# A graph layer's edge stage with its engines a whole batch apart, gathers and scatters mixed, and loads over 128 partitions

## What is computed

```python
deg = maximum(zeros(N).at[dst].add(1.0), 1.0)
edge_weight = (deg[src] * deg[dst]) ** -0.5
edge_msg = relu(edge_attr @ W1e + b1e) @ W2e + b2e
messages = (x[src] + edge_msg) * edge_weight[:, None]
agg = segment_sum(messages, dst, N)
combined = (1.0 + gin_eps) * x + agg
h = relu(combined @ W1n + b1n) @ W2n + b2n
out = h + x
out = out * rsqrt(mean(out * out, -1) + 1.19e-07) * rms_w
return layernorm(x + out)
```

## Time and profile before

| | us |
|---|---|
| median of 3 runs (2165.39 to 2170.3) | 2165.47 |
| the profiled execution, its own time | 2150.24 |
| span of that execution in the trace | 2148.5 |
| mean granted TensorE clock | 0.856 |
| PE, DVE, ACT, POOL busy in the span | 1537.2, 1290.7, 1118.8, 1303.8 |
| count stage, about | 25 to 316 |
| list set-up | 316 to 340 |
| edge stage | 340 to 1478 |
| node stage | 1484 to 2148 |

### The profile page before, as it was taken

The page is one execution under the profiler, slowest core; times in us unless marked ns, Lnnn a source line. Parts: engine busy times, 40 slices in busy tenths (PEclk is TensorE's granted clock), DMA queues, the critical chain, the costliest instruction groups (busy, mean ns, idle before and its releaser), DMA issues. The chain is left out here.

```text
span 2148.5 us, 43403 instructions
## 1 busy us (share of the span) xinstructions
PE 1537.2 (72%) x11484; PEld 1127.5 (52%) x11484; DVE 1290.7 (60%) x4579; ACT 1118.8 (52%) x3879; POOL 1303.8 (61%) x2171
## 2 busy tenths in 40 slices
PE   1114995666666667666666677775999999999993
PEld 0002554544545445445545566664777777777772
DVE  2003996333334334343333466662999999999997
ACT  1003982222222222222222244444999999999994
POOL 5772002555555555555555545553588888888888
PEclk8556997688787886877877899997999999999997
DMA  7793001212212112111111112114366666666662
GB/s 284 302 412 144 0 3 31 53 54 53 53 53 54 53 53 54 54 53 53 53 53 53 52 56 58 59 61 183 128 252 248 234 242 248 253 253 234 235 246 115
DMA packets 83038, 275.63 MB, mean 128 GB/s; under 512 B 19110, under 2 KB 46300, under 8 KB 58396
## 3 DMA queue, kind: packets, MB, share of 16 engines
q1 hardware_dynamic: 57422, 231.16, 29.2%
q0 software_dynamic: 25136, 43.60, 6.9%
q10 hardware_dynamic: 414, 0.20, 0.0%
HBM read 154.37 MB, written 128.22 MB: 132 GB/s over the span
## 5 line engine op out<-in xcount | busy, mean ns | idle before, releaser
L542 POOL DMA_INDIRECT agg_scratch<-scaled,sca_i x390 | 387.6, 994 | 576.6 <-ACT scaled L661 484.2
L1022 PE MATMUL bank<-digits,picks 128*128 128x128 f16 x5488 | 441.1, 241 | 211.7 <-DVE picks L772 121.0
L1022 PEld LDWEIGHTS bank<-digits,picks 128*128 128x128 f16 x5488 | 382.6, 110 | 319.3 <-issue 165.3
L535 POOL DMA_INDIRECT xs<-in_x,src_x x391 | 377.5, 965 | 132.4 <-issue 118.8
L886 DVE TENSOR_TENSOR msg<-bank,xs 128x512 f32<-128x512 f32 x98 | 67.8, 692 | 549.7 <-issue 536.2
L575 POOL TENSOR_SCALAR xsc<-xn,rms 128x128 f32<-128x128 f32 x784 | 277.9, 370 | 128.9 <-ACT rms L684 125.5
L655 ACT ACTIVATE he<-bank,b1e_c 128x512 f32<-128x512 f32 x98 | 67.5, 689 | 512.7 <-remote 433.3
L587 POOL TENSOR_SCALAR on<-z,neg_mean,rstd 128x128 f32<-128x128 f32 x588 | 257.2, 445 | 0.0
L1000 PE MATMUL bank<-oh_hi,steps 128*128 128x512 f16 x392 | 143.6, 406 | 144.1 <-issue 125.8
L1049 PE MATMUL bank<-w2e,he 128*128 128x128 f32 x784 | 163.2, 374 | 111.9 <-ACT he L655 111.9
L1078 PEld LDWEIGHTS bank<-w2n,hn 128*128 128x128 f32 x1568 | 205.8, 191 | 70.2 <-issue 64.6
(11 more groups left out here) (145 smaller groups left out, 2601.2 us busy)
## 6 DMA issues: line engine op xcount, KB each, us to landing
agg_scratch<-zeros SPq DMA_DIRECT2D x48, 1024.0 KB
xn<-in_x SPq DMA_DIRECT2D x48, 1024.0 KB
ag<-agg_scratch SPq DMA_DIRECT2D x48, 1024.0 KB, 6.8
out<-on SPq DMA_DIRECT2D x48, 1024.0 KB, 4.9
highq<-src_high_scratch SPq DMA_DIRECT2D x98, 128.0 KB
ea<-in_edge_attr SPq DMA_DIRECT2D x97, 127.0 KB
xs<-in_x,src_x POOLq DMA_INDIRECT x391
agg_scratch<-scaled,sca_i POOLq DMA_INDIRECT x390
```

Source lines behind the costliest of these rows:

```text
L535: pool.indirect_dma_start(out=xs[:, b % XS, j, :], out_offset=None, in_=x, in_offset=bass.IndirectOffsetOnAxis(ap=src_x[:, t:t + 1], axis= ...
L542: pool.indirect_dma_start(out=agg_rows, out_offset=bass.IndirectOffsetOnAxis(ap=sca_i[:, t:t + 1], axis=0), in_=scaled[:, b % 2, j, :], in ...
L1022: last = pe.matmul(ps[s][:, j * P:(j + 1) * P], picks[:, s, c, j * P:(j + 1) * P], digits[:, d, c * P:(c + 1) * P], start=c + d == 0, stop ...
```

## The change

1. **Start-up loads.** src and dst are loaded over all 128 partitions for the columns 0 to 342 and, for the 48 columns behind them, as 112 and as 15 partitions (ROWS = 112). The previous partition's last dst (column 0 of dst_x) comes by SP, later; the next partition's first dst is part of the wider load. Only the parts that no load covers are padded first. ACT casts dst to float after the count stage.
2. **Bias.** b2 is loaded as a row on three partitions and split in three bf16 parts there by DVE, after the count loop; PE's transposes of it (L990) go.
3. **Zero stores.** Three semaphores; each store first waits for the one three before it (ZERO_FIRST is 8 instead of 12).
4. **Gathers.** XS is 40, so 160 gathers stand ahead of the first scatter. Eight slots (32 to 39) first hold the temporaries of the list set-up, so gather 128 waits for lists_ready. The other 231 gathers are spread singly over the first 362 scatters; the last DRAIN = 7 batches have none.
5. **Steps.** In step b PE turns ea(b), counts b, multiplies by W1e, and does bias and W2e of b - 1. ACT does eaT(b), weighs b - 3, he(b), ds(b - 2), and scales b - 5, in a loop of four steps. DVE picks b + 1, does the degrees of b - 1, sums b - 4 and adds msg of b - 2; DVE and SP are written out whole, with constants for registers. `scaled` has SR = 4 buffers instead of 2.
6. **Loads.** edge_attr comes in one DMA of 128 partitions for batches below 85, then as 112 + 15. xn loads wait for 78 instead of 84 batches' msg; the first ag block comes in four pieces with a semaphore each.

```diff
-    XS = 32
+    XS = 40
+    SR = 4
+    TEMPS = 8
+    DRAIN = 7
+    ROWS = (P - 1) // 16 * 16
...
+        temps = [xs[:, XS - TEMPS + k, :, :].rearrange("p j d -> p (j d)")[:, 0:T] for k in range(TEMPS)]
+        gidx, far, sca_f, eqn, new, fst, start, left = temps
...
-            sp.wait_ge(pads_set, 1)
-            sp.dma_start(src_x[0:P - 1, 0:T], src[0:(P - 1) * T].rearrange("(p t) -> p t", t=T)).then_inc(src_in, 16)
+            sp.dma_start(src_x[:, 0:LAST_P], bass.AP(src.tensor, 0, [[T, P], [1, LAST_P]])).then_inc(src_in, 16)
+            sp.wait_ge(src_padded, 1)
+            sp.dma_start(src_x[0:ROWS, LAST_P:T], bass.AP(src.tensor, LAST_P, [[T, ROWS], [1, T - LAST_P]])
...
+                    need(sp, agg_zeroed[k % ZERO_AHEAD], 16 * (k // ZERO_AHEAD))
+                    sp.dma_start(ag_main[:, c:c + w, :], zeros[:, 0:w, :]).then_inc(agg_zeroed[k % ZERO_AHEAD], 16)
...
+                if b == XS - TEMPS and j == 0:
+                    pool.wait_ge(lists_ready, 1)
...
+            beside = T - 1 - DRAIN * TB
             for t in range(T - 1):
                 scatter(t)
-                if t % TB == TB - 1:
-                    for g in range(ahead + t - TB + 1, min(ahead + t + 1, T)):
-                        gather(g)
+                for g in range(t * (T - ahead) // beside, (t + 1) * (T - ahead) // beside):
+                    if ahead + g < T:
+                        gather(ahead + g)
...
-                if live(b - 1, BATCHES):
-                    act.wait_ge(msg_ready, at(b))
-                    act.wait_ge(ds_ready, at(b))
-                    need(act, summed, (b - 2) * TB)
+                m, r = b - 3, (u - 3) % 2
+                if live(m, BATCHES):
+                    act.wait_ge(msg_ready, at(m + 1))
+                    act.wait_ge(ds_ready, at(m + 1))
+                    need(act, summed, (m - 1) * TB)
...
+                m, r, q = b - 5, (u - 5) % 2, (u - 5) % SR
+                if live(m, BATCHES):
+                    need(act, scattered[q], m // SR * 16 * TB)
...
-            run(act, BATCHES, 2, edge_step, tail=1, head=2, peel=1)
+            run(act, BATCHES, SR, edge_step, tail=5, head=3)
...
+                if live(b - 1, BATCHES):
+                    need(pe, msg_ready, b - 2)
+                    pe.matmul(ps[4 + r][:, :], ones_b[:, :], bias[:, 0, :, :].rearrange("p j d -> p (j d)"),
+                              start=True, stop=False)
+                    pe.wait_ge(h_ready, at(b))
...
-            run(pe, BATCHES, 2, edge_step, peel=EA_TAIL // 2)
+            run(pe, BATCHES, 2, edge_step, tail=1, head=2, peel=EA_TAIL // 2 + 1)
```

More of the change, by code:

```diff
@@ L215, in build @@
         sums = sb("sums", [P, 2, TB, D])
-        scaled = sb("scaled", [P, 2, TB, D])
+        scaled = sb("scaled", [P, SR, TB, D])
         early.close()
@@ L476, in load_block @@
+            sp.dma_start(agg_d[N:N + P, :], zeros[:, 0, :]).then_inc(agg_zeroed[(BLOCKS + 1) % ZERO_AHEAD], 16)
+            for b in range(2, BATCHES):
+                if b + HQ - 2 < BATCHES:
+                    high_load(b + HQ - 2)
+                edge_loads(b)
             def load_block(tile, slot, whole, view, B, landed):
@@ L631, in _ @@
             run(act, BATCHES, 2, count_step)
+            act.wait_ge(dst_in, 48)
+            act.wait_ge(before_in, 32)
+            act.activation(dst_f[:, :], dst_x[:, :], ACT.Copy).then_inc(dst_set, 1)
             act.wait_ge(lengths_ready, 2)
@@ L987, in _ @@
             last.then_inc(high_turned, 1)
-            pe.wait_ge(bias_split, 1)
-            for k in range(2):
-                last = pe.transpose(ps[7][0:3, k * D:(k + 1) * D], bias_t[:, k, :], ident[:, :])
-            last.then_inc(bias_turned, 1)
             def count_step(b, u):
@@ L1048, in edge_step @@
-                for j in range(TB):
-                    last = pe.matmul(ps[4 + s][:, j * P:(j + 1) * P], he[:, s, j * P:(j + 1) * P], w2e[:, :],
-                                     start=False, stop=j == TB - 1)
-                last.then_inc(m_done, 1)
-                if live(b + 1, BATCHES):
-                    pick_counts(b + 1, 1 - s, 3)
-            for j in range(TB):
-                pick_counts(0, 0, j)
+                s, r = u % 2, (u - 1) % 2
+                if live(b, BATCHES):
+                    pe.wait_ge(ea_in[s], at(ea_loaded(b)))
+                    need(pe, eaT_ready, b)
+                    apart(pe, pe_passed)
+                    for j in range(TB):
+                        last = pe.transpose(ps[2][0:ED, j * P:(j + 1) * P], ea[:, s, j, :], ident[:, :])
+                    last.then_inc(eaT_done, 1)
+                    pick_counts(b, s, 0)
+                    pick_counts(b, s, 1)
+                    pe.wait_ge(eaT_ready, at(b + 1))
+                    need(pe, h_ready, b)
+                    pe.matmul(ps[3][:, :], w1e[:, :], eaT[:, s, :], start=True, stop=True).then_inc(h_done, 1)
@@ new lines, in edge_step @@
+                if live(b - 1, BATCHES):
[3 more added lines that the diff above has]
+                    pe.wait_ge(h_ready, at(b))
+                    for j in range(TB):
+                        last = pe.matmul(ps[4 + r][:, j * P:(j + 1) * P], he[:, r, j * P:(j + 1) * P], w2e[:, :],
+                                         start=False, stop=j == TB - 1)
+                    last.then_inc(m_done, 1)
```

349 lines of the change are left out of this document (165 added, 184 removed).

## The result

The changed kernel takes 2178.6 us (median of 11 runs, 2170.21 to 2189.46), the kernel before 2165.34 (11 runs, 2161.61 to 2170.3): ratio 1.007, 95% interval 1.0049 to 1.009. It is slower by 0.7%, where 12% faster was forecast. Its profiled execution has a span of 2174.7 us, 26.2 more than the one before, which was a quick one (2150.24 where the 11 runs begin at 2161.61); by the medians the loss is 13.3 us.

The account below looks back on a forecast made before the run. Bound: PE's signals seen only after POOL's gather bursts, so POOL's burst and PE's wait add up. Span 2148.5 − 264.9 (last scatter sooner) − 2 (hand-over) = 1881.6, plus 1.7 and 15.2: 1898 us; own range 1850 to 1960, with rivals 1750 to 2055.

Parts of the forecast that it names:

- Part 1, start-up: Loads of src and dst over 128 partitions: first gather at 6.5 us, −11.4 us (bounds −13 to −8).
- Part 2, list set-up: Between count and lists_ready: less work on the path, net −2.5 us (bounds −3 to +1).
- Part 3, the throttle: Zero stores, three in flight: they end near 200 us, far ahead of the first scatter; cost 0.
- Part 4, the fill: Edge stage start: 32 gathers after lists_ready take 40.5 us, then 25 us (bounds 0 to 45) until the first scatter.
- Part 4, the flow: Edge stage: POOL's 8.4 us a batch; signals pass between single gathers, 25 us of stalls on 98 batches (bounds 0 to 60).
- Part 5: Hand-over to the node stage: first ag block in four pieces shortens PE's 10.61 us wait, −2 us.
- C: Edge stage: all 91 batches with gathers may be the slow kind; slower than before, 2272 or 2345 us; chance 0.08.
- B: Edge stage: single gathers still stall PE, 9.5 to 11 us a batch, 2000 to 2135 us; chance 0.17.
- D: Edge stage: loads and signals as late as now, 11.2 to 11.4 us a batch, nothing changes, 2165 us; chance 0.03.
- A: Count stage: zero stores hold PE's signals; 1740 us if all stores, 1740 to 1870 if partly; chance 0.22.

Follow-up runs that it names:

- b_loads: Kernel before with only the loads of src and dst changed, to 128 + 112 + 15 partitions: 2142.48 us, before 2152.51 (ratio 0.9953).
- a_nothr: Changed kernel without the waits between zero stores, late condition: 2168.17 us (ratio 1.0075 to the kernel before).
- l_scat: Changed kernel with its 231 late gathers replaced by scatters of a constant to unused memory, late condition: 2165.23 us, before 2153.92 (ratio 1.006).
- p_count: Changed kernel with POOL waiting for PE's count signals after every fourth of its first 128 gathers, late condition: 2084.34 us, before 2166.76 (ratio 0.962).
- c_split: Changed kernel with each 512-wide count-stage matmul cut in two, 12 matmuls and weight loads a batch instead of 8: 2158.49 us in one run, before 2153.89.
- l_burst: Changed kernel with its late gathers four behind four scatters again, late condition: 2151.04 us (ratio 0.9997 to the kernel before).
- p_edge: Changed kernel with p_count's pauses, pauses in the next 32 gathers and edge stage, later gathers in fours, prompt condition: 1699.68 us, before 1782.77 (ratio 0.953).
- l_fill: Changed kernel with each of its 231 late gathers replaced by two index fills on POOL, late condition: 2014.27 us, before 2153.89 (ratio 0.936).

## Why the prediction was wrong

- **Part 1, start-up: right.** First gather at 4.91 (forecast 6.5). PE's last matmul of the count ends at 304.5 instead of 316.0, 11.5 us sooner (forecast 11.4), and in b_loads the counts are read 12.3 us sooner.
- **Part 2, list set-up: 3 us too good, within its bounds.** From PE's last count to lists_ready it takes 24.0 us before and 24.5 now (forecast −2.5, bounds −3 to +1). Behind the counts read 2.4 us are saved, but the bias operations in front run on DVE from 303.9 to 307.5, and PE is done at 304.5: they had been counted as if DVE's idling of 0.8 us covered them.
- **Part 3, the throttle: right**, by a_nothr.
- **Part 4, the fill: near.** First scatter 72.8 us behind lists_ready, forecast 40.5 + 25. PE's steps after the train took 5.8 us, but fewer got done inside it than the two counted: PE stood from 362.7 to 372.9.
- **Part 4, the flow: the step that failed.** The prediction put 25 us of stalls, bounds 0 to 60. POOL waited 348.2 us for scaled, 315 of them after the first scatter. The reading behind it was that signals are late only behind gathers, so that a gap of 1.6 us between two gathers lets them pass. But 1.0 of those 1.6 us is a scatter, and a scatter counts as well (l_scat), so in a mixed train no pause is left at all. The prediction names this case itself among the signs of being wrong ("if a scatter itself delays PE's signals") and gives it no price. A real pause of 1.2 us was enough in p_count, so the length of the gap was not the fault. A second reading was off too: the 22.4 us of a batch in the count stage were taken as the delay of a signal, and by c_split they grow with the number of PE's instructions.
- **Part 5: small.** PE's wait for ag rose from 10.61 to 20.85 us instead of falling: from 1474.74 on, when PE's matmuls of the edge stage were ending (the last w2e starts at 1475.33), POOL still had 22 scatters to issue. The pieces themselves were not tested apart.
- **Rivals.** C named the outcome with the right threshold: above 11.3 us a batch the change loses, and it took 11.7, at a granted clock of 0.76. Its signs came true as well (POOL's wait for scaled over 100 us, ACT's waits "remote", the clock under 0.8). Its price, at least 12.5 us a batch and 2272 us, was too high by 93 us: a batch now has 2.55 gathers and not the four of the old slow ones, which by the sum under l_burst makes the difference. B had the cause nearest, single gathers that still hold PE, but expected the gaps of 2.9 us to let a signal through, and its 9.5 to 11 us a batch were too few. D's 2165 is nearer to the measured 2178.6 than any other figure, by luck: the times were not unchanged, a later start and a shorter flow nearly cancelled. A is refuted by p_count; its figure of 1740 for a kernel whose PE is never held back is near the prompt 1700.

The condition does not explain the miss: the trace the prediction rests on and the result were both late. Prompt, the same forecast of 1898 would have been 197 us too high, since its count stage carries the holes.

## What to carry to other kernels

Do not judge a train of indirect DMAs by one instruction's delay: look how many instructions of the other engine pass during it, and vary that number. Where one engine issues DMAs for long without a break while another does many short instructions, try a wait on that other engine's progress after every four DMAs: here it cost nothing in the prompt condition (p_edge), and in the late one it took 93 us off the count stage (p_count). And time the unchanged kernel in every job: 1780 and 2155 us were the same code.

## What the runs showed of the hardware

- In the late condition, while POOL issues indirect DMAs with only 0.30 us between them, signals of PE come late: in the count stage one batch's signal passes in 22.4 us for 16 PE instructions and in 33.6 for 24 (c_split), that is 1.4 us for each, though PE's matmuls of a batch are done in 3 us. In the edge stage PE ran freely for the first 6.5 us of a train, and then its own instructions started only 0.7 or 1.4 us apart, a few at a time.
- A pause of 1.2 us after each four DMAs prevents it in the count stage (p_count).
- Gathers and scatters do it alike (l_scat); index fills on POOL do not (l_fill). DVE's and ACT's own instructions are not slower: one picks takes 374 ns on average late and 378 prompt, one scaled 392 and 386 in the median.
- It is there in some jobs and absent in others, on the same chip (13, 15). What decides that, and what it is that each PE instruction waits for or leaves behind, stays open; no run here could choose the condition.
